# Expert tiles of 128 rows instead of 256, routing cut into pieces, scans in thirds: one change to a graph-transformer-expert kernel

## What is computed

```
x: 6250 rows of 256; 100000 edges between them, sorted by target
xn  = layernorm(x)
gnn = xn + relu(xn @ Wself.T + segment_sum(softmax_over_edges(leaky_relu(att)) * (xn @ Wfunc.T)[src], dst))
mix = linear-attention block with feed-forward on xn
x   = x + gnn + mix
f   = layernorm(x)
g   = softmax(relu(f @ rw1 + rb1) @ rw2 + rb2)              # six experts
top_w, top_i = top_k(g, 2);   w = softmax(top_w)
y_e = relu(relu(f @ W1[e] + b1[e]) @ W2[e] + b2[e]) @ W3[e] + b3[e]
out = x + sum over the two chosen experts of w * y_e
```

## Time and profile before

| what | value |
|---|---|
| median of 3 runs | 2362.42 us (2362.23 to 2367.72) |
| the profiled execution | 2368.69 us |
| its span in the profile | 2366.5 us |
| PE busy | 1938.8 us (82%) |
| DVE busy | 1606.7 us (68%) |
| POOL busy | 1467.5 us (62%) |
| ACT busy | 650.0 us (27%) |
| softmax over the edges | 440 to 488 us |
| steps | 488 to 1780 us |
| phase c | 1781 to 1935 us |
| tiles (first layer 1 to end of last layer 3) | 1948.8 to 2320.4 us |
| tail | 2320.4 to 2366.5 us |

### The profile page before, as it was taken

How to read it: one execution, slowest core, us unless ns; L and a number is a source line. 1 busy time by engine, 2 the same in 40 slices (tenths; PEclk the granted TensorE clock), 3 DMA queues, 4 the chain that set the end, 5 groups by cost and what they waited for, 6 DMA issues and landing times.

```text
span 2366.5 us, 40522 instructions
## 1 busy us (share of the span) xinstructions
PE 1938.8 (82%) x10761; PEld 1500.8 (63%) x10761; DVE 1606.7 (68%) x3977; ACT 650.0 (27%) x2607; POOL 1467.5 (62%) x1188
## 2 busy tenths in 40 slices
PE   6899799678888887888777788888777759999992
PEld 5555688566666666666655566666554448888881
DVE  7997799877777776766667677776656762235263
ACT  2444688431111111111111111111103324443330
POOL 5000566688888888888888888878860377135164
PEclk9999555589999999999999999999988869999996
DMA  8887888445455454455444444554449646346363
GB/s 212 263 258 217 287 291 290 139 129 127 124 149 141 125 125 125 127 152 138 125 124 125 124 125 124 148 143 126 116 115 230 176 132 168 107 134 184 110 187 96
DMA packets 313504, 375.02 MB, mean 158 GB/s; under 512 B 117025, under 2 KB 267020, under 8 KB 310295
## 3 DMA queue, kind: packets, MB, share of 16 engines
q1 hardware_dynamic: 170604, 230.72, 32.3%
q0 software_dynamic: 135840, 136.92, 24.0%
q10 hardware_dynamic: 6975, 6.40, 0.9%
HBM read 281.65 MB, written 91.09 MB: 158 GB/s over the span
## 4 chain that ended last, share of the span: by engine, by line
PE 43%; issue 13%; DVE 11%; DMA 5%; POOL 3%; DVEq 3%; SPq 1%; ACT 1%; POOLq 0%; ACTq 0%
PE bank L671 41%; DMA wexp<-func_rows,a_src 5%; DVE acc L1795 4%; POOL wexp L635 2%; DVEq L1558 1%; DVE onehot L1782 1%; SPq L363 1%; PE bank L1020 1%; POOL g_all L658 1%; DVEq L1795 1%; DVE work L1574 1%; DVE work L1601 1%; DVE work L1577 1%; DVE acc L1939 0%; DMA work<-mix_rows 0%
## 5 line engine op out<-in xcount | busy, mean ns | idle before, releaser
L635 POOL DMA_INDIRECT wexp<-func_rows,a_src x850 | 1068.2, 1257 | 259.0 <-issue 199.0
L671 PE MATMUL bank<-wexp,onehot 125*125 125x257 f32 x1700 | 540.3, 419 | 240.9 <-DVE acc L1795 133.7
L1795 DVE TENSOR_TENSOR acc<-bank,acc 125x257 f32 x850 | 354.4, 417 | 386.7 <-PE bank L671 232.5
L671 PEld LDWEIGHTS bank<-wexp,onehot 125*125 125x125 f32 x1700 | 305.5, 199 | 412.7 <-issue 326.7
L1782 DVE TENSOR_SCALAR onehot<-iota_r,a_rel,a_hi 125x125 f32<-125x125 f32 x850 | 322.6, 383 | 0.0
L603 POOL TENSOR_TENSOR work<-iota_h,a_hi 125x500 f32<-125x500 f32 x85 | 109.2, 1285 | 248.6 <-PE bank L708 166.2
L658 POOL DMA_INDIRECT g_all<-y_d,work x100 | 127.0, 1270 | 212.5 <-DMA y_d<-g_all 111.1
L671 PE MATMUL bank<-g_all 128*128 128x256 f32 x1040 | 237.9, 382 | 7.4 <-DVE g_all L2081 4.2
L671 PEld LDWEIGHTS bank<-g_all 128*128 128x128 f32 x1040 | 193.9, 191 | 32.8 <-issue 7.4
L671 PE MATMUL bank<-w_s,work 128*125 128x256 f32 x800 | 206.8, 405 | 0.0
L648 POOL DMA_INDIRECT sorted_d<-acc,work x100 | 120.9, 1209 | 132.7 <-DVE acc L1939 102.8
(11 more groups left out here) (274 smaller groups left out, 2759.1 us busy)
## 6 DMA issues: line engine op xcount, KB each, us to landing
wexp<-lr_d SPq DMA_DIRECT2D x85, 625.0 KB
wexp<-in_attr SPq DMA_DIRECT2D x25, 896.0 KB
g_all<-sorted_d SPq DMA_DIRECT2D x65, 256.0 KB
y_d<-g_all SPq DMA_DIRECT2D x65, 256.0 KB
wexp<-func_rows,a_src POOLq DMA_INDIRECT x850
sorted_d<-spare SPq DMA_DIRECT2D x48, 256.0 KB
sorted_d<-spare SPq DMA_DIRECT2D x24, 384.0 KB
work<-xn_rows SPq DMA_DIRECT2D x38, 224.0 KB
```

Source lines behind the costliest of these rows:

```text
L635: pool.indirect_dma_start(ring[:, z, 0:D], None, func_rows, bass.IndirectOffsetOnAxis(ap=a_src[:, n // CS, n % CS:n % CS + 1], axis=0)).th ...
L671: return pe.matmul(o, l, r, start=first, stop=last_, **kw)
L1795: v.tensor_tensor(to, bank[3 + z % 2][0:R, 0:D + 1], to, ALU.add).then_inc(s("summed"), 1)
```

## The change

1. The tile has 128 rows instead of 256, and the parts have 9, 10 and 6 groups. The buffers get 41 + 45 + 29 = 115 tiles. The experts' indices are read eight tiles at a time. The transposes use one bank of PSUM instead of two in turn, which frees bank 1 for `ranks(1)` and `ranks(2)`.
2. `route(1)` and `route(2)` leave phase c. Each is cut into nine pieces, and DVE does at most one piece after the `tile_rows` of a tile: part 1's after tiles 0, 2, 3, ... 9, part 2's after tiles 11, 13, 14, ... 20. `route(0)` stays whole in phase c, one iteration earlier (13).
3. The blocks are combined evenly over the tiles from the sixth of a part on (18 blocks over 39 tiles, then 20 over 23), instead of two after each tile from the third on.
4. Each scan is done in three pieces of 417, 417 and 416, and its first operand, the table `reset`, is copied into three banks of PSUM by ACT beforehand.

```
-T = 256
-PARTS = (10, 9, 6)
+T = 128
+JT = T // 128
+BACK = 6
+IDS = 8
+PARTS = (9, 10, 6)
+ROUTE0 = (None, 0, 11)
+RANKS_IN = (6, 1, 1)
...
-            z = k - TILE0[p]
-            return [b[a] for a in range(max(0, 2 * (z - 2)), max(0, min(2 * (z - 1), len(b))))]
+            z, m = k - TILE0[p] - BACK, TILES[p] - BACK
+            return [] if z < 0 else [b[a] for a in range(z * len(b) // m, (z + 1) * len(b) // m)]
...
             def tile_turn(k):
-                freed(pe, s("g_xT"), k - 1)
+                freed(pe, s("g_xT"), k)
                 for c in range(2):
-                    for j in range(2):
-                        last = pe.transpose(ph(k % 2)[:, c, j * 128:(j + 1) * 128], g_x[k % 3][:, j, c * 128:(c + 1) * 128],
+                    for j in range(JT):
+                        last = pe.transpose(ph(0)[:, c, j * 128:(j + 1) * 128], g_x[k % 3][:, j, c * 128:(c + 1) * 128],
...
-                        last = mm(ph(2 + k % 2)[:, o, :], g_w1[k % 2][:, c, o * 128:(o + 1) * 128],
-                                  g_xT[k % 2][:, c, :], c == 0, c == 1)
+                        last = mm(ph(2 + k % 2)[:, o, 0:T], g_w1[k % 2][:, c, o * 128:(o + 1) * 128],
+                                  g_xT[k % 2][:, c, 0:T], c == 0, c == 1)
...
+                for p in range(1, len(PARTS)):
+                    if i == ROUTE0[p] + 7:
+                        ranks(p)
...
+            act.wait_ge(s("selected"), QS)
+            for k in range(3):
+                a, b = THIRDS[k]
+                act.activation(bank[5 + k][0:QS, 0:b + 1 - a], reset[:, a:b + 1], ACT.Copy).then_inc(s("reset_in"), 1)
...
             def scans(first, last_, between=lambda: None):
-                x_.did(v.tensor_tensor_scan(f_l, reset[:, 0:LROW], e_l, first, ALU.add, ALU.max))
-                between()
-                x_.settle()
...
+                for k, (a, b) in enumerate(THIRDS):
+                    x_.did(v.tensor_tensor_scan(f_l[:, a:b], bank[5 + k][0:QS, 0:b - a], e_l[:, a:b],
+                                                first if k == 0 else f_l[:, a - 1:a], ALU.add, ALU.max))
+                    if k == 0:
+                        between()
+                    x_.settle()
...
                 tile_rows(i)
                 for b in after_tile(i):
                     combine(b)
+                for p in range(1, len(PARTS)):
+                    z = i - ROUTE0[p]
+                    if z == 0:
+                        route_scores(p)
+                    if z == 2:
+                        route_shares(p)
+                    if z == 3:
+                        route_best(p, 0)
+                    if z == 4:
+                        route_best(p, 1)
+                    if z == 5:
+                        route_counts(p)
+                    if z == 6:
+                        route_weights(p)
+                    if z == 7:
+                        route_starts(p)
+                    if z == 8:
+                        route_tiles(p)
+                    if z == 9:
+                        route_slots(p)
```

More of the change, by code:

```diff
@@ L995, in _ @@
                     logits(i - 4)
-                for p in range(len(PARTS)):
-                    if i == GROUP0[p] + PARTS[p] + 4 - (p == len(PARTS) - 1):
-                        ranks(p)
+                if i == PARTS[0] + 4:
+                    ranks(0)
             experts = {}
@@ new lines, in wide, with along, each, row @@
+            def wide(p, a):
+                return a[:, 0:count(p) * EXPERTS].rearrange("p (b k) -> p b k", k=EXPERTS)
+            def along(p, k):
+                return rx[:, k][:, 0:count(p), None].to_broadcast([R, count(p), EXPERTS])
+            def each(p, a):
+                return a[:, None, :].to_broadcast([R, count(p), EXPERTS])
+            def row(p, k):
+                return rx[:, k, 0:count(p)]
+            def blocks_in(p, a):
+                return a[:, 2 * GROUP0[p]:2 * GROUP0[p] + count(p), :]
@@ L1984, in route, with route_best @@
-                v.tensor_tensor(row(3), row(1), row(0), ALU.subtract).then_inc(s("r_dve"), 1)
-                o.did(v.tensor_tensor(m, wide(r_oh[0]), wide(r_oh[1]), ALU.add))
+            def route_best(p, k):
+                oh, pr = wide(p, r_oh[k]), wide(p, r_pr)
+                o.did(v.tensor_reduce(row(p, k), pr, AX.X, ALU.max))
+                o.settle()
+                o.did(v.tensor_tensor(oh, pr, along(p, k), ALU.is_equal))
+                o.settle()
+                o.did(v.tensor_tensor(oh, oh, each(p, six[:]), ALU.mult))
+                o.settle()
+                o.did(v.tensor_reduce(row(p, 2), oh, AX.X, ALU.min))
+                o.settle()
+                o.did(v.tensor_tensor(oh, each(p, six[:]), along(p, 2), ALU.is_equal))
+                o.settle()
+                if k == 0:
+                    o.did(v.scalar_tensor_tensor(pr, oh, -2.0, pr, ALU.mult, ALU.add))
+                    o.settle()
+                else:
+                    v.tensor_tensor(row(p, 3), row(p, 1), row(p, 0), ALU.subtract).then_inc(s("r_dve"), 1)
@@ L2039, in _ @@
                     keep_logits(i - 4)
-                for p in range(len(PARTS)):
-                    if i == GROUP0[p] + PARTS[p] + 4 - (p == len(PARTS) - 1):
-                        route(p)
+                if i == PARTS[0] + 4:
+                    route_scores(0)
+                    route_shares(0)
+                    route_best(0, 0)
+                    route_best(0, 1)
+                    route_counts(0)
+                    route_weights(0)
+                    route_starts(0)
+                    route_tiles(0)
+                    route_slots(0)
             picked = {}
```

122 lines of the change are left out of this document (62 added, 60 removed).

## The result

| | before | changed |
|---|---|---|
| median | 2365.07 us (2362.23 to 2369.39) | 2344.61 us (2339.56 to 2347.84) |
| ratio | 1 | 0.990, 95% interval 0.988 to 0.992 |
| the profiled execution, its span | 2366.5 us | 2343.3 us |

The account below looks back on a forecast made before the run. POOL was taken to bound the softmax and steps, DVE phase c, PE the tiles. The terms -6 - 23 - 38.7 + 8 - 0.5 = -60.2 us, on the median of 2362.4, gave 2302 us, range 2288 to 2328.

Parts of the forecast that it names:

- Scans: Softmax: with one scan operand in PSUM the gathers are no longer held up, -6 us (bounds -7.7 and 0).
- the ring holds 34: Softmax and first steps: POOL gets about 4 gathers ahead and just fits; +1 us if the ring makes it wait.
- Phase c: Before the tiles: without `route(1)` and `route(2)` the first layer 1 starts at 1924.6 to 1928 instead of 1948.75, -23 us.
- The pieces: Between tiles: routing work moved into DVE's slack costs 0 to 2 us; `ranks` on PE costs 1 us.
- SP's order: In the tiles: a tile's load stands behind a block's stores and has about 2.5 us to land; priced within the stalls.
- The tiles: PE's tile period falls from 5.62 to 2.84 us, 326.6 us for 115 tiles against 365.3, -38.7 us.
- The rivals of 0.125 and of 0.19 us a record: PE's tiles: records take 0.125 us, 2334 us in all, chance 0.07; or 0.19 as weight loads show, 2451, slower 0.03.
- Stalls: In the tiles: combined blocks and register loads make PE wait, 0 to 25 us, taken as +8, mostly in part 2.
- DVE or SP sets the period: Tiles with combined blocks or register loads are paced by DVE or SP: 27 us instead of 8, 2321 us, chance 0.15.
- the rival that names sends: Start of the tiles: the sends or the phase c pace stay late, +9 us, 2311; within the forecast's 0.70.

Follow-up runs that it names:

- part 4 alone: The kernel before with only the scans done in thirds, first operand in PSUM: 2366.3 against 2370.9 us, ratio 0.9985 (0.9974 to 0.9996).
- the kernel without the three causes: The changed kernel with aligned index reads, SP's block stores after the next load, and no sends of parts 1 and 2 (output wrong): 2307.5 us, ratio 0.973.
- part 2 undone: The changed kernel with all of `route(1)` and `route(2)` back in phase c: 2362.8 us, ratio 0.997 (0.995 to 0.998).

## Why the prediction was wrong

- **Scans, -6**: right in mechanism; the gathers beside them now take 1.21 us and POOL gains 6.1 us by the 31st gather. The sentence "some 30 are issued before the first step, and the ring holds 34, so this just fits" failed. The ring is full three times, and by the 101st gather 0.3 to 4.8 us are left, 3.6 (1 to 6) by the medians of part 4 alone. The range that I gave, -7.7 to 0, holds it. The Trainium skill, SBUF — State Buffer, Who interferes with whom, infers that a tensor_tensor with two SBUF inputs doesn't stall the making of descriptors; here the long gathers vanished when one operand went to PSUM, and the gather at 477.16 that still takes 2.49 lies beside L1790, a tensor_tensor of 1.46 us with both inputs in SBUF, which starts at 477.11 by DVE's timeline, so the trace disagrees.
- **Phase c, -23**: measured -21.3. First send 1860.94 (forecast 1861.6), first load 1918.02 (1919), layer 1 at 1923.89 (1924.6 to 1928 without the scans' share). Right.
- **The pieces, 0 to 2, and one more for `ranks`**: right where no sends lie beside them: with reads, sends and SP's order out of the way both cost 2 us. Beside the sends their share isn't known.
- **The tiles, -38.7**: right. The period is 2.87 (forecast 2.84), 3.5 us over 115 tiles, and the tiles without stalls take 335.6 us (332.9). The rivals of 0.125 and of 0.19 us a record are excluded. The Trainium skill, TensorE: Matmul & The Clock Gate, The mechanism, by which each record's weight load would show, is contradicted for 128 columns as it was for 256 by the trace of before: 0.11 us a record, weights and all.
- **Stalls, +8 (0 to 25)**: this is the term that failed. The changed kernel loses 34.8 us more than the kernel without the three causes. Two steps led to it. First, the reads: "there are 16 loads where there were 18" counts them and doesn't ask what a read of eight costs, though the change says eight. It is 1.9 us instead of 1.0, where the sum took 0.8 from the earlier trace rows, it is made by three engines in turn, and the slack that had hidden it was halved by the same change: 11.5 us. Second, the sends stood nowhere in the sum except for whether they end in time. Moving `route(1)` and `route(2)` into the tiles puts all 64 sends of parts 1 and 2 behind the first layer 1, where 47 stood before: 16.7 us, in other executions more, with long reads, late signals and at times the lower clock as its parts. The clock stood nowhere in the sum either. SP's order, 6.6 us, is what I had priced, in the place where I had put it. The range's end of 25 rested on blocks and reads of 0.8 us and so was too low as well.
- **The rivals**: none was the one that happened. "DVE or SP sets the period" (2321) names two of the three causes: it gave 19 us to blocks, where SP's order cost 6.6, and 16 x 0.5 = 8 to reads, which cost 11.5. The sends beside the tiles, half of the loss, are in none: the rival that names sends means those in front of the first tile.

Two pages that I had not weighed bear on a price for the reads. The Trainium skill, DMA: Bandwidth & Descriptors, Latency and other measured facts, gives a tensor_load a floor of about 600 ns. The trace disagrees: aligned reads of eight take 0.60 to 0.62, but aligned reads of four 0.38 and a read of one value 0.31. The Trainium skill, Runtime: NRT & Kernel Launch, Instruction fetch mechanics, says about 200 ns a register, of loads that fetch registers from HBM; for the reads of SBUF here, those of eight that aren't aligned (1.93, 0.24 a value) agree roughly, the aligned ones (0.08 a value) don't. An estimate by that page's figure would have been 1.6 us for eight, and the doubling foreseen.

## What to carry to other kernels

When a change halves a loop's period, list everything that happens once per iteration or once per few, with its duration, and hold each against the new slack, not the old: what was hidden by 5.6 us isn't by 2.9. When work is moved off a serial stretch, the asynchronous work that depends on it moves too, and it must be priced where it lands. When one stretch varies by 10 us and more from execution to execution, two repairs can each measure as nothing and give 1% together; causes are then best judged by the stretch of the trace on which they act, beside the unrepaired kernel measured in the same session, and by taking all away at once.

## What the runs showed of the hardware

- A read of SBUF values into registers costs 0.24 us a value (four 0.97, eight 1.93) when it starts 8, 12, 24 or 28 bytes behind a multiple of 32, and 0.60 for eight and 0.38 for four when it starts at one; four that start 16 bytes behind one are as short. Beside POOL's scatters the long reads of eight take up to 4.5 us, and 2.2 at most without them.
- Beside POOL's scatters PE's signals to ACT and DVE can come up to 5.7 us late (ACT's and DVE's starts against PE's ends; the usual distance is 0.14 to 0.16), while signals to PE don't. It varies by execution of one program: tiles 10 to 30 took 70.5, 78.9 and 85.0 us. With the sends partly in phase c (part 2 undone) such waits are 3.3 us in all. The cause is open.
- After such stalls the granted clock can be at its lower level (0.50 from 2010.2 to 2017.0 us, behind an idle PE), and 16 records then take 3.75 us instead of 1.97.
- A scan with one operand in PSUM and one in SBUF doesn't lengthen the gathers beside it (1.21 us); with two in SBUF it does (2.56 and 3.19).
